# State read-outs of odd batches through the off-diagonal 32x32 tiles of TensorE

## What is computed

```python
def step(s, inp):                       # s: state of a head, 16 x 16
    q_, w_, k_, v_, a_, b_ = inp
    sa = einsum('bhij,bhj->bhi', s, a_)
    s = s * w_[:, :, None, :] + sa[..., None] * b_[:, :, None, :] + v_[..., None] * k_[:, :, None, :]
    return s, einsum('bhij,bhj->bhi', s, q_)      # the read-out y
_, y = jax.lax.scan(step, s0, (qt, wt, kt, vt, at, bt))
...                                     # group norm of y by head, bonus, gate, output projection
x = layernorm(x + attn(x)); x = layernorm(x + moe(x))
```

## Time and profile before

| | |
|---|---|
| median of three runs | 1264.62 us |
| profiled execution | 1266.16 us, span 1264.3 us |
| TensorE's granted clock, mean | 0.877 |
| PE matmul / weight load busy | 1069.8 us (85%) / 861.9 us (68%) |
| DVE / ACT / POOL busy | 798.7 (63%) / 625.1 (49%) / 720.6 us (57%) |
| L633 matmul records | 2048 |
| chain that ended last | PE 63%, ACT 14%, issue 11%, DVE 8%, DMA 2% |

### The profile page before, as it was taken

The page is one execution under the profiler, slowest core; times in us unless marked ns, Lnnn a source line. Parts: engine busy times, 40 slices in busy tenths (PEclk is TensorE's granted clock), DMA queues, the critical chain, the costliest instruction groups (busy, mean ns, idle before and its releaser), DMA issues.

```text
span 1264.3 us, 42014 instructions
## 1 busy us (share of the span) xinstructions
PE 1069.8 (85%) x16514; PEld 861.9 (68%) x16515; DVE 798.7 (63%) x1752; ACT 625.1 (49%) x1213; POOL 720.6 (57%) x1138
## 2 busy tenths in 40 slices
PE   3668788997898998989979889876548999999996
PEld 2436666776666677777667666665348988888885
DVE  2575676686776856767576776622246666666663
ACT  1463485785865856758566685633302222222221
POOL 1076976986968779677796787872011333333331
PEclk9689897898998978879888998887559999999998
DMA  3013032241240331413404133036733544444440
GB/s 89 17 26 78 11 77 57 41 93 45 52 94 12 86 80 18 93 20 77 94 3 93 22 76 85 17 79 181 251 122 123 192 167 167 163 161 166 159 147 8
DMA packets 208623, 111.98 MB, mean 89 GB/s; under 512 B 172364, under 2 KB 191952, under 8 KB 208080
## 3 DMA queue, kind: packets, MB, share of 16 engines
q1 hardware_dynamic: 204720, 101.29, 29.3%
q0 software_dynamic: 3744, 8.40, 2.0%
HBM read 85.41 MB, written 26.08 MB: 88 GB/s over the span
## 4 chain that ended last, share of the span: by engine, by line
PE 63%; ACT 14%; issue 11%; DVE 8%; DMA 2%; SPq 1%; DVEq 0%; POOL 0%; ACTq 0%; POOLq 0%
PE bank L530 13%; PE bank L820 10%; PE bank L833 7%; PE bank L602 7%; PE ry L633 4%; PE ry L833 3%; PE bank L610 3%; PE bank L558 3%; PE bank L567 2%; PE ry L639 2%; PE bank L671 2%; PE ry L682 2%; PE bank L655 2%; ACT arena L874 2%; ACT L960 1%
## 5 line engine op out<-in xcount | busy, mean ns | idle before, releaser
L1672 POOL TENSOR_TENSOR arena<-arena 128x30 f32<-128x30 f32 (+14 forms) x480 | 320.3, 667 | 37.6
L1669 POOL TENSOR_TENSOR arena<-arena 128x30 f32<-128x30 f32 (+14 forms) x480 | 299.0, 623 | 36.4
L530 PE MATMUL bank<-arena 128*128 128x256 f32 (+2 forms) x992 | 287.4, 433 | 34.4 <-DMA arena<-in_centT 13.9
L530 PEld LDWEIGHTS bank<-arena 128*128 128x128 f32 x992 | 188.5, 210 | 85.7 <-issue 31.3
L820 PEld LDWEIGHTS bank<-arena 128*128 128x128 f32 x1248 | 146.2, 194 | 5.4 <-DVE arena L1568 2.6
L820 PE MATMUL bank<-arena 128*128 128x128 f32 x1248 | 147.5, 277 | 2.0 <-DVE arena L1568 2.0
L602 PEld LDWEIGHTS bank<-arena 32*128 32x128 f32 x2048 | 88.5, 257 | 40.5 <-issue 40.3
L1312 DVE TENSOR_TENSOR arena<-bank,arena 128x512 f32<-128x512 f32 x128 | 80.7, 682 | 55.2 <-PE bank L602 55.2
L602 PE MATMUL bank<-arena 32*128 32x64 f32 x2048 | 94.6, 348 | 20.1 <-DVE arena L1290 12.5
L610 PE MATMUL bank<-arena 128*128 128x128 f32 x576 | 91.0, 299 | 14.1 <-ACT arena L1037 7.7
L610 PEld LDWEIGHTS bank<-arena 128*128 128x128 f32 x576 | 72.6, 154 | 38.9 <-issue 19.2
(11 more groups left out here) (164 smaller groups left out, 1920.1 us busy)
## 6 DMA issues: line engine op xcount, KB each, us to landing
arena<-in_W SPq DMA_DIRECT2D x47, 1024.0 KB, 5.0
scr_n<-arena SPq DMA_DIRECT2D x64, 128.0 KB, 2.6
arena<-scr_n SPq DMA_DIRECT2D x16, 512.0 KB, 3.4
scr_u<-arena SPq DMA_DIRECT2D x16, 512.0 KB, 2.7
arena<-scr_u SPq DMA_DIRECT2D x64, 128.0 KB, 2.8
arena<-in_xTp SPq DMA_DIRECT2D x32, 132.0 KB, 4.0
arena<-in_x SPq DMA_DIRECT2D x64, 64.0 KB, 2.8
scr_x<-arena SPq DMA_DIRECT2D x64, 64.0 KB, 2.0
```

Of the source, the lines that this page charges most:

```text
L530: mm = pe.matmul(ring.tile(m, name)[0:rows, to], lhsT, rhs, start=(i == 0), stop=(i == len(terms) - 1))
L1669: inv_ok.inc(f"m{s}", TT(t, U[:, 0:s, s:s + 1].broadcast_to(shape), U[:, s:s + 1, s + 1:TB].broadcast_to(shape), ALU.mult))
L1672: inv_ok.inc(f"a{s}", TT(U[:, 0:s, s + 1:TB], U[:, 0:s, s + 1:TB], t, ALU.add))
```

## The change

The result of an odd batch's read-out for pair p goes to the partitions of pair (p + 2) mod 4. Even batches stay. L655 reads RT at the columns that answer to it, and keep_y moves the halves of y back with one instruction for even batches and two of 64 partitions for odd ones; every wait for "ye", "yo" also has the third name "yp".

```diff
-        chain_act = Stage(sem("chain_act"), [(-1, "rt0 rt1 x0e x1e ye yo")])
+        chain_act = Stage(sem("chain_act"), [(-1, "rt0 rt1 x0e x1e ye yo yp")])
...
+            def ry_rows(b, p):
+                return slice(32 * ((p + 2 * (b % 2)) % PAIRS), 32 * ((p + 2 * (b % 2)) % PAIRS) + 32)
+
...
-                    chain_act.wait(pe, m - 1, "ye", "yo")
+                    chain_act.wait(pe, m - 1, "ye", "yo", "yp")
...
-                            pe.matmul(RY[b % 2][r, f * 4 + b // 2], S[r, f * B + b, :], aq[buf][r, f * B + b],
+                            pe.matmul(RY[b % 2][ry_rows(b, p), f * 4 + b // 2], S[r, f * B + b, :], aq[buf][r, f * B + b],
...
-                            mm = pe.matmul(RY[b % 2][r, f * 4 + b // 2, 0], XV[buf][v, f * B + b, r],
+                            mm = pe.matmul(RY[b % 2][ry_rows(b, p), f * 4 + b // 2, 0], XV[buf][v, f * B + b, r],
...
-                                           RT[f][x, k, 32 * p:32 * p + 32], start=True, stop=True)
+                                           RT[f][x, k, ry_rows(e, p)], start=True, stop=True)
...
-                            mm = pe.matmul(RY[b % 2][r, f * 4 + b // 2, 1], XV[buf][:, f * B + b, r], sc[buf][:, f, p, b // 2, b % 2, 1],
+                            mm = pe.matmul(RY[b % 2][ry_rows(b, p), f * 4 + b // 2, 1], XV[buf][:, f * B + b, r], sc[buf][:, f, p, b // 2, b % 2, 1],
...
-                for e, name in enumerate("eo"):
-                    chain_act.inc(m, f"y{name}", A(to[:, :, e], RY[e][:, :, 1], ACT.Copy))
+                chain_act.inc(m, "ye", A(to[:, :, 0], RY[0][:, :, 1], ACT.Copy))
+                for i, name in enumerate(("yo", "yp")):
+                    chain_act.inc(m, name, A(to[64 * i:64 * i + 64, :, 1], RY[1][64 * (1 - i):64 * (1 - i) + 64, :, 1], ACT.Copy))
```

More of the change, by code:

```diff
@@ L498, in _ @@
                     load_experts()
-            chain_act.wait(sp, last, "ye", "yo")
+            chain_act.wait(sp, last, "ye", "yo", "yp")
             for i, n in enumerate(("ln_g", "ln_b", "b2")):
@@ L686, in centre_y @@
             def centre_y(m):
-                chain_act.wait(pe, m, "ye", "yo")
+                chain_act.wait(pe, m, "ye", "yo", "yp")
                 fill(m, "yc", [(all_cols, [(centre, flat(yc))])])
```

## The result

The changed kernel takes 1287.16 us (median of 4 runs, 1282.05 to 1293.42), the kernel before 1262.29 (4 runs). The ratio is 1.0216, with a 95% interval of 1.0167 to 1.0264: slower by more than 1%. 1282 was predicted. The profiled execution is 1293.42 us, with a span of 1291.5 for 1264.3, and the mean granted clock is 0.840 for 0.877.

The account below looks back on a forecast made before the run. PE was taken to bound the kernel, with the supply of instruction packets as second limit. 1266.16 us profiled, -8 -1 +0.3 +26, gave 1283, and 1282 for the median, 1.5 below the profiled execution; range 1254 to 1293.

Parts of the forecast that it names:

- (1): L633 (now L636) in the read-out: eight tiles instead of four save 0.8 us a run at half clock, 0.44 at full.
- (2): Read-out: instruction packets 3.7 us apart let one run's saving of two count, 8 us at half clock plus 1 at full.
- (3): L639 (now L642) keeps eight tiles and L655 (now L658) only reads other columns: nothing gained or lost.
- (4): L682 (now L685): changed column-group order costs at most 0.4 us a block, covered by the gap of L682 and L671.
- (5): keep_y's third ACT instruction: hidden except in the last block, where PE waits 0.3 us more.
- (6): Behind half-clock read-outs: seven of eight returns to full clock are lost, 3.7 us each, 26 us in all.
- the clock is gained: Rival, behind seven low-clock read-outs: eight tiles hold the clock, 3.7 us back each, 1243 or 1230 us; chance 0.12.
- the gain is kept: Rival, read-outs: the 9 us saving stays and the clock is as before, 1256 us; chance 0.19.
- nothing happens: Rival, L633's tiles: those of one row group don't overlap or only four stay in flight, 1265 us; chance 0.11.
- Loads in line: Rival, L633's batch changes: weight loads wait for the streaming row group, 1.0 us a run, 16 us, 1281 us; chance 0.06.

Follow-up runs that it names:

- e3: Kernel before, all tiles on the diagonal, with L633 reading the state out for the first kind of read only (32 columns instead of 64): 1298.6 us, ratio 1.0207.
- e1: Changed kernel with L636 taking the four even batches first, then the four odd ones, meant to keep four tiles in flight: 1273.9 us, ratio 1.0055.
- c1 to c4: centre_y moved mid-read-out plus unneeded matmuls a block: six on before, six on changed, four on changed, four on before; ratios 0.9984, 1.0021, 1.0052, 1.0021.
- f3: Kernel before with centre_y moved between the read-out's halves and two unneeded 384-column matmuls added in the read-out: 1276.6 us, ratio 1.0072.
- f4: Changed kernel with centre_y moved between the read-out's halves and two unneeded 384-column matmuls added in the read-out: 1273.2 us, ratio 1.0064.
- e5: Kernel before with 16 unneeded 256-column matmuls added a block, in read-out, read_out and update: 1298.9 us, ratio 1.0249.
- c4: Kernel before with centre_y moved between the read-out's halves and four unneeded matmuls a block added in read_out and update: 1271.5 us, ratio 1.0021.
- f1: Kernel before with only centre_y's needed matmul moved from behind the read-out to between its halves, nothing added: 1258.7 us, ratio 0.9931.
- e4: Changed kernel with 16 unneeded 256-column matmuls added a block, in read-out, read_out and update: 1288.1 us, ratio 1.0162.

## Why the prediction was right

By its own steps:

(1) L636 at half clock: forecast some 1.1 us a run for 1.93, measured 1.18. At full clock a run of 64 takes 0.85 us, where 0.65 was forecast:

```profile
516.37 0.85 PE L636 MATMUL ry<-arena 32*32 32x64 f32 x64
517.16 0.33 PE L642 MATMUL ry<-arena 64*32 64x32 f32 x25
519.36 0.68 PE L642 MATMUL ry<-arena 64*32 64x32 f32 x39 [1.87 <-issue]
...
523.09 0.68 PE L642 MATMUL ry<-arena 64*32 64x32 f32 x39 [1.58 <-issue]
```

(0.85 - 0.21) / 63 = 10.2 ns a record; 14.0 was not halved. It cost nothing here, since the gaps took the rest.

(2) The supply: from gap end to gap end 523.09 - 519.36 = 3.73 us, to the hundredth that of the earlier trace rows, at a half-clock second run here and a full-clock one there. That packets of instructions end these gaps, the prediction inferred from the count of records; the DMA packets in the trace bear it out. In the blocks of the kernel before PE has 42 gaps with "issue" as the only cause, and each ends 1.2 to 1.5 us after a packet of 16,384 bytes has landed on the instruction queue. But 3.7 us is not the least time between two of them, as the prediction had it. The kernel before has a shorter one too, 451.56 - 448.09 = 3.47 us with a gap at both ends, and its packets start 3.28 us apart at the least:

```profile
448.09 0.31 PE L639 MATMUL ry<-arena 64*32 64x32 f32 x2 [0.29 <-issue]
448.33 1.93 PE L633 MATMUL ry<-arena 32*32 32x64 f32 x64
450.19 0.87 PE L639 MATMUL ry<-arena 64*32 64x32 f32 x62
451.56 0.31 PE L639 MATMUL ry<-arena 64*32 64x32 f32 x2 [0.50 <-issue]
```

The term of what is kept was mis-sized: 9 us were taken, 2 were measured. The mean read-out, over the first 15, is 5.97 us for 6.10. The reason is in the first timeline above: the first run gave 0.75 us, but the gap grew by 0.85, and the second L642 ran at 0.89 for 0.76, since the clock was still down. The prediction let the clock act only behind the read-out; in the kernel before it had come back inside it.

(3) and (4) L642 and L685: L642 is 0.89 for 0.89. L685 takes 9.1 ns a record for 8.5, 0.07 us a read_out, under the bound of 0.4:

```profile
243.70 1.36 PE L685 MATMUL ry<-arena 128*32 128x32 f32 x128 [1.17 <-DVE arena L1332]
```

(5) keep_y: in the last block the three copies take 0.38 + 0.78 us (the two 64-partition ones cost as much each as one of 128), and PE waits 1.34 us for them where it waited 0.81: 0.5 us for the 0.3 forecast. ACT's timeline of the changed kernel, to be held against the earlier trace rows, and PE's, changed and before:

```profile
909.77 0.38 ACT L1027 ACTIVATE arena<-ry 128x256 f32<-128x256 f32 x1 [4.94 <-PE ry L685]
910.18 0.78 ACT L1029 ACTIVATE arena<-ry 64x256 f32<-64x256 f32 x2
```

```profile
911.01 2.08 PE L530 MATMUL bank<-arena 128*128 128x512 f32 x2 [1.34 <-ACT arena L1029]
```

```profile
884.65 2.07 PE L530 MATMUL bank<-arena 128*128 128x512 f32 x2 [0.81 <-ACT arena L1025]
```

(6) The clock: seven of eight returns were forecast lost, at 3.7 us each, 26 us; all eight were lost. The stretch from the read-out's end to the first L658 grew from 24.56 to 26.23 us in the mean of 15 blocks: 25 us. That is within a microsecond of the term, and in part by luck: two errors in it offset each other. One return more was lost than forecast, and behind the eight read-outs that had their return before, the stretch grew, block by block, by 23.6 us together, 2.9 each and not 3.7; in the first block it was only 0.15. The stretches of the other seven blocks grew by 1.5 us together.

The sum as a whole was short: it had +17 us on the profiled execution, and the two profiled executions are 27 apart (the medians 25). By the trace it is -2 from the read-outs and +25 from the stretch behind them. The other 4 us were, but for keep_y's 0.5, in no term: 3.3 in the stretch from L658 to the next read-out, 2.6 behind the start of the last read-out (keep_y's 0.5 is in it), which starts at half clock in the changed kernel and at full clock in the kernel before, and -1.8 ahead of the first.

One reading under step (6) was too simple. It set long runs of 1.93 us apart from short runs with waits. But the read-outs from 445 and 498 of the kernel before have the long runs too, and stay at half clock, with PE busy for 6.12 of 6.90 and 5.74 of 6.30 us. The first read-out, with 4.91 of 5.90, got the clock back. So how long PE streams in a read-out does not decide by itself; that it counts is shown by e3 and e1, and what else decides is open.

Of the rivals, the changed kernel's own trace rules out that the clock is gained or stays as it was (277 us at half clock for 175), and the ratio that the gain is kept. e3 shows that the loss needs no tile off the diagonal. That nothing happens is ruled out by the run of 1.18 us. Loads in line is ruled out by the same run: at 13.8 ns a record the 8 records of a batch take 110 ns, less than one load of L636 (145 ns in the median), so these loads did not wait for the tile beside them. Here the off-diagonal tiles of one row group loaded and streamed beside each other.

What is not settled: why the added matmuls of c1 to c4 and f3, f4 gave less than forecast is argued from their length in the timeline and from the half-clock times in the table, not shown by a run that changes the length alone. Nor is it settled why f3's did not bring the clock back. e5 has more of them, in read_out and update too; and c4, which has them only there, starts every read-out but the first at full clock, where f1 and f3 start 13 and 10 of their 16 at half.

## What to carry to other kernels

Before making a stretch of small matmuls faster, see what limits it next: here a packet of instructions every 3.3 to 4 us for 128 matmul records. Under this limit the faster tiles only turned streaming into standing still (a run of 1.18 us for 1.93, a gap of 1.17 for 0.32), and here that cost the clock for what followed, over ten times what the tiles gave (25 us for 2). Put large matmuls that are needed anyway between runs of small ones: it adds no work, fills the wait, and was worth 0.7% on the kernel before and 2.8% on the changed one. Matmuls that nobody needs are no substitute: e4 and e5 had the full clock nearly throughout (36 and 33 us at half clock) and were 1.6% and 2.5% slower than the kernel before.

## What the runs showed of the hardware

Tiles (p, p) and (p, p+2), in one row group and in different column groups, ran at once: 64 records of 64 columns in 1.18 us at half clock for 1.93, and in 0.85 us at full clock for 1.09. For the granted clock, eight tiles at once for half the time were no substitute for four tiles for the whole: it came back in eight of ten half-clock read-outs with the four and, in the profiled execution, left none of sixteen read-outs at full clock with the eight. PE's instructions came in packets of 16,384 bytes, 128 matmul records with their loads (19 + 64 + 45 from gap to gap in the earlier trace rows). In the kernel before no two of them start within 3.28 us, and PE waits for them 4.0 us a block. And a kernel that leaves work out was slower for it: half the columns in one line, +2.07%.
